# Unread identity transposes on TensorE at the head and before six waits, and one group's statistics moved behind its keys, in a two-phase graph-layer kernel

## The chip, the cores and the metric

One core of one Trainium2 chip runs the program. The metric is the time of one execution on the device in microseconds (us). The engines are named as the profile names them: PE (TensorE, matrix products and transposes into PSUM), DVE (VectorE), ACT (ScalarE), POOL (GpSimd) and SP (SyncE, which here only issues DMAs). PEld is the loading of the stationary operand on PE. The profile gives the clock that PE was granted as a share of full speed: 1.00 is 2.4 GHz, 0.50 is 1.2 GHz.

## The reference

The reference is one layer over 12500 nodes with 256 features. Cut to what matters:

```python
xn  = layernorm(x)
# graph part: 4 heads of 64 features, the neighbour of node n is col[n]
xt  = xn @ weight
al  = softmax(leaky_relu(sum(xt[row]*attn_l) + sum(xt[col]*attn_r)), over heads)
gnn = broadcast(sum over heads of al[n, h] * xt[col[n], h])
# linear attention, 8 heads of 32
Q, K = elu(xn @ Wq) + 1, elu(xn @ Wk) + 1
msg = (Q @ (K^T @ V)) / (Q . sum(K) + eps);  msg = layernorm(msg @ Wm)
h   = relu(concat(xn, msg) @ W1) @ W2;       x = x + gnn + xn + layernorm(h)
# mixture of experts on z = layernorm(x): a shared three-layer net, 4 experts, top 2
x   = x + shared(z) + sum over the 2 best experts of weight * expert(z)
```

The attention's sum over all nodes has to be complete before the first message can be formed. That splits the kernel in two phases.

## The kernel before

The nodes are cut into 25 groups (`NG`): 24 of 512 nodes (4 tiles of 128 rows) and a last one of 212 (2 tiles of 106). Every engine has its own instruction stream, written out by hand and ordered by semaphores; an engine executes its stream in that order, so a wait holds back all that is written behind it.

**The head** brings in group 0 and the first weights: DVE takes statistics of the rows (`stats`, `aggregate`), POOL turns them into scale and shift (`rstd`), ACT normalizes (`p1_norm`, result `xn1`), PE transposes (`p1_transpose`), ACT and DVE split the result in a high and a low part (`x1T_hi`, `x1T_lo`).

**Phase 1** then takes one group `v` a turn. PE's turn is: keys (`p1_k`, which needs `x1T_lo` of the group), transposes of group v+1 (which need `xn1` of v+1), and for each of two pairs of tiles the node tables (`p1_table`) and the sum of keys times rows of the group before (`p1_kx`, which needs POOL's `xr_lo` and `k_lo`). ACT's turn is: exponential of the keys (`kf`), copy of the transposed group v+1 (`x1T_hi`), two table copies (`xts`), normalization of group v+2. DVE's turn is: `xr_hi`, the statistics of group v+2 (`p1_stats`), the two operations on `kf`, `x1T_lo` of v+1, `k_hi`. POOL's turn is: `xr_lo`, `rstd` of group v+2, `k_lo`.

**The seam** between the phases (240 to 345 us) finishes the sum (`kx`), turns it (`kxT`), forms `kvT`, its product with `Wm` and a folded W1 weight, and runs turns 0 to 2 of phase 2 in an order of their own (`turn0`, `turn1`, and `phase2` with `second=True`).

**Phase 2** takes one group a turn: W1, W2, message, gating, shared net and experts. `w2_pair(i, 1)` waits for the four expert activations `e1` of ACT.

Each product of two fp32 operands is done as three products of parts in a faster type (`split_mm`, lines 282 to 284).

Of the kernel before, what the change touches and what calls it, by code (L numbers as in the profile page):

```python
# [20 lines left out]
P = 128  # L21
# [3 lines left out]
NG = -(-N_NODES // GR)  # L25
# [39 lines left out]
def gps_layer(nc, A):  # L65

    ctx = ExitStack()
    with ctx:
# [59 lines left out]
        ident = sb("ident", [P, P])  # L128
# [124 lines left out]
        psum = ctx.enter_context(nc.psum_tensor("psum", [P, 8, BANK], F32))  # L253
# [232 lines left out]
        def _(pe):  # L486
            def transposes(src, b, done, norm=None, before=0, t=T):
# [7 lines left out]
                                            ident[0:R, 0:R])  # L495
                last.then_inc(S[done], 1)

            def tile(t, c, j):
                return t[:, c, j * R:(j + 1) * R]

# [8 lines left out]
            def p1_transpose(v, par):  # L509
                if due(v):  # L510
                    pe.wait_ge(S["x1T"], v)
                transposes(xn1[par], 0, "x1t", "xn1", T * v, tiles(v))
# [36 lines left out]
            def phase1(v, par, kx=True, more=True):  # L549
                p1_k(v, par)  # L550
                if more:
                    p1_transpose(v + 1, 1 - par)
                for pair in range(2):
                    p1_table(v, par, pair)
                    if kx:
                        p1_kx(v - 1, 1 - par, pair, first=isinstance(v, int) and v == 1)

            def hidden(name, chunk, o, b, x, n=CK, t=T):

                for c in range(n):  # L560
                    last = split_mm(pe, colT(b, t=t), (wslice(w_hi, name, chunk + c, o * P, P),
                                                       wslice(w_lo, name, chunk + c, o * P, P)),
                                    (x[0][:, c, 0:t * R], x[1][:, c, 0:t * R]), c == 0, c == n - 1)
                return last
# [15 lines left out]
            def p2_expand(i, bank=6):  # L580
                pe.wait_ge(S["den_rows"], i + 1)
                for q in range(CK):
                    pe.matmul(colT(bank + q, t=tiles(i)), den_sel[:, q, :], rdenT[:, 0:tiles(i) * R], start=True,  # L583
                              stop=True).then_inc(S["dx"], 1)
# [11 lines left out]
            def w1_part(half, o, b, x, t=T):  # L596

                for c in range(CK):
                    k = 2 * half + c
                    last = split_mm(pe, colT(b, t=t),  # L600
                                    (wslice(w_hi, "W1", k, o * P, P), wslice(w_lo, "W1", k, o * P, P)),
                                    (x[0][:, c, 0:t * R], x[1][:, c, 0:t * R]), k == 0, k == 3)
                return last
# [6 lines left out]
                return last  # L610

            pe.wait_ge(S["ident"], 1)
            for half, done in enumerate(("x1t_first", "x1t")):
                for j in range(2):
                    pe.wait_ge(S["xn1"], 2 * half + j + 1)
                    for c in range(CK):
                        last = pe.transpose(psum[:, 4 * half + c, j * R:(j + 1) * R],
                                            xn1[0][:, 2 * half + j, c * P:(c + 1) * P], ident[0:R, 0:R])
                last.then_inc(S[done], 1)
            pe.wait_ge(S["wk_split"], 1)  # L620
            pe.wait_ge(S["x1T_first"], 1)
            first_k(0)
            pe.wait_ge(S["x1T"], 1)
            first_k(1).then_inc(S["k_mm"], 1)
            p1_transpose(1, 1)
            pe.wait_ge(S["w_split1"], 1)
            for pair in range(2):
                p1_table(0, 0, pair)
            phase1(1, 1)
            steps(pe, phase1, 2, NG - 2)  # L630
            phase1(NG - 2, (NG - 2) % 2)
            phase1(NG - 1, (NG - 1) % 2, more=False)
            pe.wait_ge(S["w_later"], 16 * LATER_LOADS)
            for o in range(4):
                for c in range(CK):
# [7 lines left out]
                p1_kx(NG - 1, (NG - 1) % 2, pair, last=True)  # L643


            pe.wait_ge(S["kxs"], 1)
            pe.wait_ge(S["xts"], 2 * NG)
            for c in range(CK):
                for q in range(CK):
                    last = pe.transpose(psum[:, 4 + c, q * P:(q + 1) * P], kx[:, q, c * P:(c + 1) * P], ident[:])  # L650
            last.then_inc(S["kxt_mm"], 1)
            pe.wait_ge(S["kden"], 1)
            p2_den(0)
            pe.wait_ge(S["kxT"], 1)
# [3 lines left out]
                                     kxT[:, c, q * P:(q + 1) * P], start=c == 0, stop=c == CK - 1)  # L658
            last.then_inc(S["kv_mm"], 1)
            w1_part(0, 0, 4, (xT_hi[0], xT_lo[0]))  # L660
            p2_expand(0)
            pe.wait_ge(S["kvT"], 1)
            for q in range(CK):
# [8 lines left out]
            def w2_pair(i, pair):  # L672

                if pair == 0:
                    pe.wait_ge(S["s1_relu"], 2 * (i - 1))
                else:
                    pe.wait_ge(S["e1_relu"], 4 * (i - 1))
                for j in (2 * pair, 2 * pair + 1):
                    for k in range(4):
                        last = split_mm(pe, rowt(0, j), (tile(h_hi, k, j), tile(h_lo, k, j)),  # L680
                                        (wslice(w_hi, "W2", k), wslice(w_lo, "W2", k)), k == 0, k == 3)
                last.then_inc(S["w2"], 1)
# [19 lines left out]
            def phase2(i, par, second=False):  # L702
# [29 lines left out]
                for e in range(EXPERTS):  # L732
                    if e == 1:
                        pe.wait_ge(S["s1_relu"], 2 * (i - 2) + 1)
                        pe.wait_ge(S["lg"], i - 1)
                        pe.transpose(psum[0:R, 5, 0:P], logitsT[:], ident[:]).then_inc(S["lt_mm"], 1)
                    hidden("eW1", 2 * e, 0, E1_BANKS[e], zT).then_inc(S["e1_mm"], 1)
                pe.wait_ge(S["h_lo"], 2 * i)
                for pair in range(2):
                    w2_pair(i, pair)  # L740
                pe.wait_ge(S["gate_rows"], i - 1)
                pe.transpose(psum[:, 5, 0:R], flat(scale_rows), ident[0:R, 0:R]).then_inc(S["scale_t"], 1)  # L742
# [514 lines left out]
        def _(dve):  # L1257
# [25 lines left out]
                now = slice(0, t * R)  # L1283
                tt(x1T_lo[par][:, :, now], colT(0, 2, t), x1T_hi[par][:, :, now], ALU.subtract).then_inc(S["x1T"], 1)

            def phase1(v, par, more=2):
                if due(v - 1):
                    dve.wait_ge(S["kx"], v - 1)
                t = tiles(v)
                dve.wait_ge(S["xn1"], xn_done(v + 1))  # L1290
                if isinstance(v, int) and v < 2:
                    dve.wait_ge(S["xr_ones"], 1)
                dve.tensor_copy(xr_hi[par][:, 0:t, 0:C], xn1[par][:, 0:t, :]).then_inc(S["xr_hi"], 1)
                if more >= 2:
                    p1_stats(v + 2, par)
                dve.wait_ge(S["k_exp"], v + 1)
                k = kf[par][:, 0:t, :]
                ts(k, k, 1.0, None, ALU.min)
                dve.drain()
                stt(k, rows4(2, t), 1.0, k, ALU.add, ALU.max).then_inc(S["kf"], 1)  # L1300
                if more >= 1:
                    p1_lowT(v + 1, 1 - par)
                dve.drain()
                dve.tensor_copy(k_hi[par][:, 0:t, :], k).then_inc(S["k_hi"], 1)

            dve.wait_ge(S["x_first"], 32)
            stats(LX[0], (0, 1), lambda j: xb[0][:, j, :])
# [21 lines left out]
            dve.tensor_copy(wx_hi[:, :, 0:XA_W], wx_raw[:])  # L1329
            dve.drain()  # L1330
            tt(wx_lo[:, :, 0:XA_W], wx_raw[:], wx_hi[:, :, 0:XA_W], ALU.subtract).then_inc(S["w_split1"], 1)
            phase1(0, 0)
            phase1(1, 1)
            steps(dve, phase1, 2, NG - 3)

# [76 lines left out]
            for q in range(CK):  # L1412
                at = kden[:, q, :].rearrange("p (d n) -> p d n", n=MIX_HEADS)[:, :, q * per:(q + 1) * per]
# [582 lines left out]
```

## Time and profile before

| | us |
|---|---|
| median of 3 runs | 1332.97 (1332.23 to 1333.31) |
| profiled execution, own time | 1329.47 |
| its span from first to last instruction | 1327.7 |
| PE busy | 1294.9 (98%) |
| DVE busy | 1045.5 (79%) |
| ACT busy | 751.7 (57%) |
| POOL busy | 646.3 (49%) |
| mean granted clock of PE | 0.993 |

Busy times are sums over the span of one profiled execution. Its own time is 1.8 us over its span and 3.5 us under the median of the runs without a profile.

### The profile page before, as it was taken

Reading aid. Unit: us, or ns where it says so; the run is one execution under the profiler, and the core shown is the slowest. Engines: PE = TensorE matmul, PEld = TensorE weight load, DVE = VectorE, ACT = ScalarE, POOL = GpSimd, SP = SyncE. Lnnn points to the kernel's source line nnn. Section 1 sums busy time; section 2 is a strip of 40 time slices with the busy share of each in tenths; the row PEclk is TensorE's granted clock in tenths of the full one; section 3 lists DMA queues with packets and bytes.
Section 4 is the critical chain, followed back from the end, with each engine's and each line's share of the span. In section 5 each row is a group of like instructions: output and inputs, shape, how many; then the busy total and the mean of one; then the engine's idle time right before and its main releaser. Section 6 shows DMA issues by size and latency. Waiting matters only on the chain.

```text
span 1327.7 us, 25928 instructions
## 1 busy us (share of the span) xinstructions
PE 1294.9 (98%) x8730; PEld 1122.8 (85%) x8730; DVE 1045.5 (79%) x2383; ACT 751.7 (57%) x1520; POOL 646.3 (49%) x721
## 2 busy tenths in 40 slices
PE   6999999898999999999999999999999999999998
PEld 6999999776888888888888888888888888888876
DVE  6887777878778787787878788787877878787765
ACT  4555555344557565565646565575645656565654
POOL 6777777636344443444343453444434453434421
PEclk9999999899999999999999999999999999999999
DMA  6787767522122312122021220222111220212000
GB/s 207 241 288 246 250 224 236 150 61 71 28 69 68 80 45 59 56 80 80 25 79 56 80 76 28 68 67 80 46 58 56 80 80 24 80 56 71 25 16 24
DMA packets 65459, 123.23 MB, mean 93 GB/s; under 512 B 31725, under 2 KB 36176, under 8 KB 65422
## 3 DMA queue, kind: packets, MB, share of 16 engines
q1 hardware_dynamic: 57422, 109.25, 25.5%
q0 software_dynamic: 8000, 13.53, 4.4%
q8 instruction: 19, 0.31, 0.1%
q14 instruction: 18, 0.15, 0.0%
HBM read 70.41 MB, written 52.32 MB: 92 GB/s over the span
## 4 chain that ended last, share of the span: by engine, by line
PE 89%; DVE 5%; ACT 2%; issue 1%; DVEq 1%; POOL 1%; DMA 0%; POOLq 0%; SPq 0%; ACTq 0%
PE psum L282 26%; PE psum L284 25%; PE psum L283 25%; PE psum L698 3%; PE psum L494 3%; PE psum L751 1%; PE psum L689 1%; PE psum L576 1%; PE psum L761 1%; PE psum L583 1%; PE psum L505 1%; DVE s_lo L1580 0%; DMA xb<-in_x 0%; DVE mT_lo L1553 0%; DVE qm L1547 0%
## 5 line engine op out<-in xcount | busy, mean ns | idle before, releaser
L1904 POOL TENSOR_TENSOR h_lo<-relu,h_hi 128x1024 fp32r<-128x1024 f32 (+1 forms) x50 | 124.0, 2481 | 170.6 <-ACT h_hi L1027 170.6
L282 PE MATMUL psum<-w_hi,h_hi 128*128 128x256 f32 x588 | 166.2, 283 | 3.6 <-ACT e L1038 3.1
L284 PE MATMUL psum<-w_hi,h_lo 128*128 128x256 f32 x588 | 165.8, 282 | 0.0
L283 PE MATMUL psum<-w_lo,h_hi 128*128 128x256 f32 x588 | 165.6, 282 | 0.0
L1904 POOL TENSOR_TENSOR s_lo<-relu,s_hi 128x512 fp32r<-128x512 f32 x23 | 29.7, 1293 | 206.7 <-ACT s_hi L1140 206.7
L282 PE MATMUL psum<-z_hi,w_hi 128*128 128x512 f32 (+1 forms) x300 | 121.7, 406 | 1.3 <-DVE z_lo L1673 1.0
L1060 ACT ACTIVATE mT_hi<-qm 128x1024 fp32r<-128x1024 f32 x23 | 24.4, 1062 | 170.5 <-DVE qm L1547 170.5
L282 PE MATMUL psum<-xT_hi,w_hi 128*128 128x512 f32 (+1 forms) x300 | 118.6, 395 | 0.2 <-DVE relu L1620 0.2
L1898 POOL DMA_INDIRECT xg<-table_xt,idx x100 | 100.0, 1000 | 35.6 <-issue 31.9
L284 PE MATMUL psum<-z_hi,w_lo 128*128 128x512 f32 (+1 forms) x300 | 116.2, 387 | 0.0
L284 PE MATMUL psum<-xT_hi,w_lo 128*128 128x512 f32 (+1 forms) x300 | 116.2, 387 | 0.0
L283 PE MATMUL psum<-xT_lo,w_hi 128*128 128x512 f32 (+1 forms) x300 | 116.1, 387 | 0.0
L283 PE MATMUL psum<-z_lo,w_hi 128*128 128x512 f32 (+1 forms) x300 | 116.0, 387 | 0.0
L282 PEld LDWEIGHTS psum<-w_hi,h_hi 128*128 128x128 f32 x588 | 111.3, 189 | 5.4 <-ACT e L1038 3.3
L283 PEld LDWEIGHTS psum<-w_lo,h_hi 128*128 128x128 f32 x588 | 112.6, 191 | 0.9
L1900 POOL DMA_INDIRECT ag<-table_al,idx x100 | 97.8, 978 | 30.5 <-issue 30.5
L284 PEld LDWEIGHTS psum<-w_hi,h_lo 128*128 128x128 f32 x588 | 111.2, 189 | 0.0
L1038 ACT ACTIVATE e<-psum,e_bias 128x512 f32<-128x512 f32 (+1 forms) x100 | 67.7, 680 | 49.8 <-PE psum L284 48.8
L1520 DVE SCALAR_TENSOR_TENSOR base<-xb,rn,b_bc 128x256 f32<-128x256 f32 x98 | 92.0, 981 | 0.2 <-issue 0.2
L1032 ACT ACTIVATE scaleT<-psum 32x128 fp32r<-32x128 f32 x98 | 26.4, 269 | 113.8 <-PE psum L742 112.9
L282 PE MATMUL psum<-mT_hi,w_hi 128*128 128x512 f32 (+1 forms) x200 | 80.0, 400 | 2.9 <-DVE mT_lo L1553 2.9
L284 PE MATMUL psum<-mT_hi,w_lo 128*128 128x512 f32 (+1 forms) x200 | 78.1, 390 | 0.0
(279 smaller groups left out, 4242.9 us busy)
## 6 DMA issues: line engine op xcount, KB each, us to landing
xb<-in_x SPq DMA_DIRECT2D x47, 448.0 KB, 4.0
xT_hi_table<-x1T_hi SPq DMA_DIRECT2D x25, 512.0 KB, 2.9
xT_lo_table<-x1T_lo SPq DMA_DIRECT2D x25, 512.0 KB, 3.6
xT_hi<-xT_hi_table SPq DMA_DIRECT2D x25, 512.0 KB
xT_lo<-xT_lo_table SPq DMA_DIRECT2D x25, 512.0 KB
table_xt<-xts SPq DMA_DIRECT2D x24, 455.0 KB, 3.0
out<-xmid SPq DMA_DIRECT2D x24, 448.0 KB
xb<-in_x SPq DMA_DIRECT2D x47, 64.0 KB, 4.1
```

What stands on the lines that cost most here:

```text
L282: pe.matmul(out, wh, xh, start=first, stop=False)
L283: pe.matmul(out, wh, xl, start=False, stop=False)
L284: return pe.matmul(out, wl, xh, start=False, stop=last)
L494: last = pe.transpose(psum[:, b + c, j * R:(j + 1) * R], src[:, j, c * P:(c + 1) * P], ident[0:R, 0:R])
L698: last = pe.matmul(psum[m * HEAD_CH:(m + 1) * HEAD_CH, 2 + q, 0:t * R], second_w[:, e, :], e1[:, e, 0:t * R], start=True, stop=True)
L1032: last = act.activation(scaleT[0:QUAD, j * R:(j + 1) * R], psum[j * QUAD:(j + 1) * QUAD, 5, 0:R], ACT.Copy)
L1038: act.activation(e1[:, e, 0:t * R], colT(bank, t=t), ACT.Relu, bias=e1_bias[:, e:e + 1]).then_inc(S["e1_relu"], 1)
L1060: act.activation(mT_hi[:], qm[:], ACT.Copy).then_inc(S["mT_hi"], 1)
L1520: last = stt(base[:, j, :], xb[par][:, j, :], rn2[par][:, 0, j:j + 1], b2_bc[:], ALU.mult, ALU.add)
L1898: pool.indirect_dma_start(xg[par][:, j, :], None, table_xt.ap(), bass.IndirectOffsetOnAxis(idx[par][:, 1, j:j + 1], 0)).then_inc(S[f"gath{ ...
L1900: pool.indirect_dma_start(ag[par][:, j, :], None, table_al.ap(), bass.IndirectOffsetOnAxis(idx[par][:, 0, j:j + 1], 0)).then_inc(S[f"gath{ ...
L1904: ptt(out, src, hi, ALU.subtract).then_inc(S[done], 1)
```

## The change

`keep_clock(n, bank)` issues n transposes of the identity matrix into a PSUM bank. Nothing reads their result, and they wait for nothing of their own. They are put at ten places of PE's stream: 38 as soon as the identity exists, 8 after each half of group 0's transposes, 8 ahead of the wait for the split of the table weights, and then 9, 14, 7, 6, 9 and 24 at the seam, ahead of the waits for POOL's `k_lo`, `kxs`, `kden`, `den_rows`, `h_lo` and `e1_relu`. On DVE, `p1_stats` of group 2 goes from behind `xr_hi` of group 0 to behind `k_hi` of group 0. All other turns are as before.

```diff
+            def keep_clock(n, bank, at=0):
+
+                for _ in range(n):
+                    pe.transpose(psum[:, bank, at:at + P], ident[:], ident[:])
+
...
             pe.wait_ge(S["ident"], 1)
+            keep_clock(38, 6)
             for half, done in enumerate(("x1t_first", "x1t")):
...
                 last.then_inc(S[done], 1)
+                if half == 0:
+                    keep_clock(8, 6)
+            keep_clock(8, 6)
             pe.wait_ge(S["wk_split"], 1)
...
             p1_transpose(1, 1)
+            keep_clock(8, 6)
             pe.wait_ge(S["w_split1"], 1)
...
-            phase1(NG - 1, (NG - 1) % 2, more=False)
+            p1_k(NG - 1, (NG - 1) % 2)
+            for pair in range(2):
+                p1_table(NG - 1, (NG - 1) % 2, pair)
+                if pair == 0:
+                    keep_clock(9, 1)
+                p1_kx(NG - 2, NG % 2, pair)
...
+            keep_clock(14, 1)
             pe.wait_ge(S["kxs"], 1)
...
             last.then_inc(S["kxt_mm"], 1)
+            keep_clock(7, 1)
             pe.wait_ge(S["kden"], 1)
...
             w1_part(0, 0, 4, (xT_hi[0], xT_lo[0]))
+            keep_clock(6, 5)
             p2_expand(0)
...
+                if second:
+                    keep_clock(9, 3)
                 pe.wait_ge(S["h_lo"], 2 * i)
                 for pair in range(2):
+                    if second and pair == 1:
+                        keep_clock(24, 3)
                     w2_pair(i, pair)
...
-            def phase1(v, par, more=2):
+            def phase1(v, par, more=2, stats_last=False):
...
-                if more >= 2:
+                if more >= 2 and not stats_last:
                     p1_stats(v + 2, par)
...
                 dve.tensor_copy(k_hi[par][:, 0:t, :], k).then_inc(S["k_hi"], 1)
+                if more >= 2 and stats_last:
+                    p1_stats(v + 2, par)
...
-            phase1(0, 0)
+            phase1(0, 0, stats_last=True)
             phase1(1, 1)
```

The stream of PE at the head, before the change, begins with the transposes of group 0 (`xn_0`):

```order
L617 MATMUL psum<-ident,xn_0 128x128 [waits s_xn1,s_ident]
L617 MATMUL psum<-ident,xn_0 128x128
L617 MATMUL psum<-ident,xn_0 128x128 [waits s_xn1]
L617 MATMUL psum<-ident,xn_0 128x128
L617 MATMUL psum<-ident,xn_0 128x128 [waits s_xn1]
```

With the change the same place reads:

```order
L501 MATMUL psum<-ident 128x128 [waits s_ident]
L501 MATMUL psum<-ident 128x128 x37
L623 MATMUL psum<-ident,xn_0 128x128 [waits s_xn1]
L623 MATMUL psum<-ident,xn_0 128x128
L623 MATMUL psum<-ident,xn_0 128x128 [waits s_xn1]
L623 MATMUL psum<-ident,xn_0 128x128
L501 MATMUL psum<-ident 128x128 x8
L623 MATMUL psum<-ident,xn_0 128x128 [waits s_xn1]
```

The 38 identity transposes wait for the identity alone, and group 0's transposes keep their waits for `xn1` behind them.

PE's stream at the end of phase 1, before, goes from the last key product (`k_hi`, `k_lo`) to the turning of the sum `kx` and on to the denominators (`kden`):

```order
L284 MATMUL psum<-xr_hi,k_lo 128x258
L650 MATMUL psum<-ident,kx 128x128 [waits s_xts,s_kxs]
L650 MATMUL psum<-ident,kx 128x128 x3
L576 MATMUL psum<-qf,kden 32x128 [waits s_q,s_kden]
L576 MATMUL psum<-qf,kden 32x128 x7
L657 MATMUL psum<-w_raw,wv 128x128 [waits s_kxT]
```

With the change:

```order
L284 MATMUL psum<-xr_hi,k_lo 128x258
L501 MATMUL psum<-ident 128x128 x14
L666 MATMUL psum<-ident,kx 128x128 [waits s_xts,s_kxs]
L666 MATMUL psum<-ident,kx 128x128 x3
L501 MATMUL psum<-ident 128x128 x7
L581 MATMUL psum<-qf,kden 32x128 [waits s_q,s_kden]
L581 MATMUL psum<-qf,kden 32x128 x7
L674 MATMUL psum<-w_raw,wv 128x128 [waits s_kxT]
```

Fourteen and seven identity transposes stand ahead of the two waits; nothing else moved.

DVE's stream in the turn of group 0, before, from the low part of the table weights (`wx_lo`) to the `xr_hi` of group 1 (`xn_1`):

```order
L1331 TENSOR_TENSOR wx_lo<-wx_raw,wx_hi 128x2x264
L1293 CAST xr_hi<-xn_0 128x4x256 [waits s_xr_ones,s_xn1]
L1262 BN_STATS bn_x<-xb 128x6 [waits s_rs_x1,s_x0]
L1262 BN_STATS bn_x<-xb 128x6 x3
L1267 BN_AGGR mv_x<-bn_x 128x2 x4
L1298 TENSOR_SCALAR kf<-kf 128x1024 [waits s_k_exp]
L1300 SCALAR_TENSOR_TENSOR kf<-psum,kf 128x1024
L1284 TENSOR_TENSOR x1T_lo<-psum,x1T_hi 128x1024 [waits s_x1T_hi]
L1304 CAST k_hi<-kf 128x1024
L1293 CAST xr_hi<-xn_1 128x4x256 [waits s_xr_ones,s_xn1]
```

With the change:

```order
L1355 TENSOR_TENSOR wx_lo<-wx_raw,wx_hi 128x2x264
L1315 CAST xr_hi<-xn_0 128x4x256 [waits s_xr_ones,s_xn1]
L1320 TENSOR_SCALAR kf<-kf 128x1024 [waits s_k_exp]
L1322 SCALAR_TENSOR_TENSOR kf<-psum,kf 128x1024
L1306 TENSOR_TENSOR x1T_lo<-psum,x1T_hi 128x1024 [waits s_x1T_hi]
L1326 CAST k_hi<-kf 128x1024
L1284 BN_STATS bn_x<-xb 128x6 [waits s_rs_x1,s_x0]
L1284 BN_STATS bn_x<-xb 128x6 x3
L1289 BN_AGGR mv_x<-bn_x 128x2 x4
L1315 CAST xr_hi<-xn_1 128x4x256 [waits s_xr_ones,s_xn1]
```

The statistics of group 2 (`mv_x`) have gone behind four operations, two of which wait for ACT. The streams of ACT, POOL and SP are the same as before.

## Rows read from the trace of the kernel before

**Rows 1.** Stretches: length, busy PE, PEld, DVE, ACT, POOL (instructions); clock; DMA share, GB/s.

```profile
40.00:240.00 200.00, 200.00 (x1693) 199.82 (x1693) 154.94 (x290) 113.50 (x214) 146.19 (x144) 1.00 0.76 247
345.00:1278.00 933.00, 932.65 (x6011) 786.72 (x6010) 747.47 (x1767) 546.95 (x1122) 408.50 (x462) 1.00 0.20 60
```

**Rows 2.** PE's longest waits, 240 to 345 us: total, times, longest.

```profile
PE psum L282 <- ACT e L1038: 3.1, 1, 3.1
...
PE psum L282 <- POOL k_lo L1874: 2.4, 1, 2.4
PE psum L576 <- DVE kden L1414: 1.2, 1, 1.2
PE psum L650 <- DVE kx L1409: 0.8, 1, 0.8
```

**Rows 3.** Three of the seam's four stretches at the lower clock, as rows 1.

```profile
245.10:248.50 3.40, 3.40 (x18) 3.40 (x18) 3.31 (x3) 0.28 (x2) 3.04 (x2) 0.51 0.21 66
258.80:262.30 3.50, 3.50 (x27) 2.92 (x18) 2.96 (x8) 0.00 (x0) 2.72 (x3) 0.51 0.36 68
...
333.90:337.30 3.40, 3.40 (x17) 3.40 (x17) 1.75 (x10) 0.09 (x1) 0.00 (x0) 0.50 0.02 5
```

**Rows 4.** First key products and a later stretch of them, as rows 1.

```profile
12.30:16.30 4.00, 4.00 (x19) 4.00 (x20) 3.78 (x7) 2.08 (x4) 0.79 (x3) 1.00 0.91 345
22.70:25.30 2.60, 2.60 (x23) 2.60 (x24) 2.44 (x6) 1.98 (x5) 1.93 (x1) 1.00 0.75 296
```

**Rows 5.** DVE in order of time, from 16.3 us on: start, length, instruction.

```profile
16.36 0.69 DVE L1293 CAST xr_hi<-xn 128x1024 fp32r<-128x1024 f32 x1
17.20 1.41 DVE L1262 BATCH_NORM_STATS2 bn_x<-xb 128x6 f32<-128x256 f32 x4 [0.16 <-issue]
18.68 0.38 DVE L1267 BATCH_NORM_AGGREGATE mv_x<-bn_x 128x2 f32<-128x6 f32 x4
18.98 1.09 DVE L1298 TENSOR_SCALAR kf<-kf 128x1024 f32<-128x1024 f32 x1
...
21.29 1.21 DVE L1284 TENSOR_TENSOR x1T_lo<-psum,x1T_hi 128x1024 fp32r<-128x1024 f32 x1
22.59 0.69 DVE L1304 CAST k_hi<-kf 128x1024 fp32r<-128x1024 f32 x1
...
26.76 0.75 DVE L1298 TENSOR_SCALAR kf<-kf 128x1024 f32<-128x1024 f32 x1 [0.43 <-ACT kf L969]
```

**Rows 6.** POOL: xr_lo of group 0, then group 2's scale chain, first and last.

```profile
17.12 2.40 POOL L1870 TENSOR_TENSOR xr_lo<-xn,xr_hi 128x1024 fp32r<-128x1024 f32 x1 [3.87 <-DVE xr_hi L1293]
19.48 0.65 POOL L1825 TENSOR_TENSOR veps_x<-mv_x,eps 128x4 f32<-128x4 f32 x1
...
21.86 0.20 POOL L1832 TENSOR_TENSOR rn<-nmean_x,rs_x 128x4 f32<-128x4 f32 x1
```

**Rows 7.** ACT: normalization of group 2 and exponential of group 1's keys.

```profile
22.60 2.07 ACT L944 ACTIVATE xn<-xb,rn,rs_x 128x256 f32<-128x256 f32 x4
25.70 1.03 ACT L969 ACTIVATE kf<-psum 128x1024 f32<-128x1024 f32 x1 [1.02 <-PE psum L284]
```

**Rows 8.** PE: transposes of group 2 and the table behind them.

```profile
25.50 1.03 PE L494 MATMUL psum<-ident,xn 128*128 128x128 f32 x8
26.29 0.37 PE L282 MATMUL psum<-wx_hi,x1T_hi 128*128 128x264 f32 x1
```

**Rows 9.** The seam's denominators on PE, and what stands around them on DVE.

```profile
254.45 1.23 DVE L1389 TENSOR_SCALAR qf<-psum 128x1024 f32<-128x1024 f32 x1 [1.81 <-PE psum L284]
...
258.55 0.90 PE L576 MATMUL psum<-qf,kden 128*32 128x128 f32 x16 [1.23 <-DVE kden L1414]
...
263.08 0.62 PE L583 MATMUL psum<-rdenT,den_sel 128*128 128x512 f32 x2
```

**Rows 10.** DVE's gate rows in turn 2, and PE's transpose that needs them.

```profile
335.18 0.17 DVE L1487 TENSOR_TENSOR scale_rows<-top_e,top_hi 128x16 f32<-128x16 f32 x1
...
336.75 0.41 PE L742 MATMUL psum<-ident,scale_rows 128*128 128x128 f32 x1
```

## The prediction

> **What bounds the kernel now.** I read the busy times by stretch first. In both long loops PE is busy all the time: 200.00 of 200 us in phase 1 and 932.65 of 933 us in phase 2, at the full clock [rows 1]. The reader is to see two things there: nothing in the loops can be gained by this change, which touches none of them, and whatever the head or the seam gains or loses comes out at the end whole, since PE works its stream off without a gap behind them. What is left is the head (0 to 22.6 us) and the seam (240 to 345 us). There I read PE's waits [rows 2] and the clock [rows 3]. The seam has waits of 3.1, 2.4, 1.2 and 0.8 us that the change touches, and behind them three stretches of about 3.4 us at half clock, in which PE is busy throughout; a fourth such stretch lies behind the wait for row_z of turn 2, which gets no transposes. The first key products at the head also run at the lower rate: 19 in 4.00 us, 0.21 us each, where a later stretch has 23 in 2.60 us, 0.113 each [rows 4]. (The clock column says 1.00 there; the rate of the products is what I trust.)
>
> **The price of the identity transposes.** The eight transposes of group 2 start at 25.50 and the table behind them at 26.29 [rows 8]: 0.10 us each at the full clock, so about 0.20 at half. I take the added ones at the same price. They are free where the wait behind them is longer.
>
> **Seam, wait for k_lo (9).** PE waits 2.4 us there [rows 2]; nine take 0.9 us, hidden by POOL's k_lo. Should the clock hold, the stretch 245.1 to 248.5 goes at full rate: half of 3.4 us, 1.70 us gained. Does it go through? PE's next consumer is DVE's qf, which stood idle 1.81 us for PE [rows 9], so 1.70 fits in. Term: −1.7. If nine don't hold the clock it is 0.
>
> **Seam, kxs, kden, den_rows (14, 7, 6).** The fourteen cost 1.4 us against a wait of 0.8 [rows 2]: the turning of kx starts 0.6 late. That eats into the next wait, 1.2 us, leaving 0.6 for seven transposes of 0.7 us: denominators at most 0.1 late. What the clock gives: the denominators take 0.90 us at half clock ahead of DVE [rows 9]; I take a third of it, 0.3, as back, since DVE starts on the last result. From there DVE's chain to den_rows sets the time (an addition, a reciprocal, a cast and four products, some 3.2 us), not PE's products, so their faster clock is worth only what PE was late behind that chain: PE reaches the expansion at 263.08 [rows 9]; den_rows is there some 0.35 before it by the same sum (258.55 + 0.94 + 3.2 = 262.7). Six transposes fit in the freed time. Term: −0.3 −0.35 = −0.65, bounds 0 and −1.7 (half of the whole stretch).
>
> **Seam, turn 2 (9, 24).** PE waits 3.1 us for ACT's e [rows 2]; 24 take 2.4, and the nine ahead of them push pair 0 by some 0.4 us into the same wait. Both are hidden, with 0.3 us to spare. The stretch 333.9 to 337.3 [rows 3] then runs at full rate: 1.7 at most. DVE's gate rows, needed next, are done at 335.35 and PE got to them at 336.75 [rows 10], so at that step 1.35 of 1.4 can be taken, and the expansion behind it adds 0.2. Term: −1.6.
>
> The fourth stretch I leave as it is. Seam in sum: −1.7 −0.65 −1.6 = **−3.95**.
>
> **Head, the clock.** The identity is there at about 1.75 us, group 0's rows at 9.1. 38 transposes need 38 × 0.20 = 7.6 us if the clock never rises (until 9.4, 0.3 late) and less if it does. If it has risen by 12.1, the 24 key products of group 0 are done at about 15.0 instead of 17.0, and ACT's exponential of them (1.03 us as for group 1 [rows 7]) starts at 15.4 behind its own normalization of group 1 and is done at 16.4. DVE is free at 17.05, where its xr_hi ends [rows 5]. So with the clock alone DVE would have gone on to the statistics as before and nothing would be gained: kf's first operation stood at 18.98 behind the statistics, not behind ACT. That is what the move of the statistics releases.
>
> **Head, the move.** I follow DVE's chain with the distances of rows 5. kf starts as xr_hi ends, at 17.0. It takes 0.75 as at 26.76, if it starts ahead of POOL's xr_lo (17.12), and 1.09 or more if behind. From kf to x1T_lo it was 2.31 us with the 1.09, so 1.97 with 0.75; from there to k_hi 1.30; from k_hi to the statistics 0.84, as between xr_hi and them; and 1.86 until mv_x is ready. So x1T_lo starts at 18.95 and ends at 20.15, k_hi starts at 20.25, the statistics at 21.1, and mv_x is ready at 22.95. Before, x1T_lo ended at 22.50 and mv_x was ready at 19.06 [rows 5]. So the keys of group 1 can start on PE at 20.4 (behind its second table) instead of 22.5, a gain of 2.1; and the statistics of group 2 come 3.9 us later. Who waits for them: POOL's scale chain (19.48 to 22.06 before, 2.6 us, and 2.15 if its first small operation takes 0.20 like its last and not 0.65 [rows 6]), then ACT's normalization of group 2 (2.07 [rows 7]), then PE's transposes of group 2, which had 0.8 us of slack (xn1 ready at 24.67 [rows 7], PE there at 25.50 [rows 8]). Now: 22.95 + 0.1 + 2.6 + 2.07 = 27.7 and two transposes: the table behind them at 27.95 against 26.29 [rows 8]. The gain of 2.1 at the keys is lost in a wait of about 2.3 us in front of these transposes, and **the head ends 1.65 us later**; with 2.15 for POOL's chain, 1.2 later. Queued behind ACT's late normalization is also its exponential for group 1, at 25.70 before [rows 7], now at 27.7; DVE's x1T_lo for group 2, five operations on, is there at 32, and PE needs it at 33.9, so that costs nothing more. POOL's k_lo of group 0 is behind the scale chain too, done at 28.1, needed at 29.4.
>
> And the clock: that wait has no identity transposes. PE stands from 23.4 to 25.7 and then does two transposes each half microsecond until 27.8. The wait of 2.4 us for k_lo was followed by 3.4 us at half clock [rows 2, 3]. The same here costs between 0.6 us (if most of the low stretch falls on the idle time) and 1.7. I take 1.3. Head in sum: 1.65 + 1.3 = **+2.95**, bounds +1.2 and +3.8.
>
> **Sum.** −3.95 + 2.95 = −1.0 us. On the profiled execution's 1329.5 that is 1328.5; on the median of the runs, 3.5 us higher, **1332.0**. About 0.2% (2.7 us) is what a measurement of this kernel can tell from no change, so this forecast is "the same". Its own range is −2.7 to +1.7, 1330.3 to 1334.7.
>
> **The rivals.**
>
> *The head costs little or gains; faster.* If POOL's chain takes the shorter 2.15 and the clock is not lowered in the new wait, the head is +1.2 and the sum −2.75 (1330.2). If xn1 of group 2 came in time for some reason that I don't see, the head would even be −2.1 and the sum −6 (1327). For it: the seam's gains rest on rows that are plain, and a shorter fourth stretch, by chance of its place, would add to them (up to 1.7). Against it: POOL's order puts the scale chain ahead of k_lo and ACT's puts the normalization ahead of kf, so nothing can overtake. It decides from a head below +1.3. Chance 0.28.
>
> *Nine are too few at the k_lo wait.* 0.9 us of work in 2.4 leaves 1.5 idle; the wait for kden (1.2, with 0.8 shortly ahead) was also followed by half clock. Then −1.7 is missing: +0.7, 1333.7. Also "the same". Chance 0.10.
>
> *The identity transposes don't keep the clock; slower.* The trace has no stretch with transposes alone from which this could be read: the eight of row_z in turn 2, spread out by ACT's pace, came just ahead of the fourth half-clock stretch. If they don't count, the 54 at the head run at 0.20: the 38 end at 9.4, and the 16 behind group 0's two halves add 3.2 us ahead of the first keys, so these start at about 15.0 instead of 12.1 and are at half rate. The keys end near 20, kf on DVE starts at 21.1 instead of 17.0, and all of the head comes 4.1 later than forecast: +2.95 + 4.1 = +7. The seam gains nothing. Sum +7: 1340. It decides if the first key products are at 0.21 us each. Chance 0.12. The Trainium skill, page "TensorE: Matmul & The Clock Gate", Part 4 on the PE-mode transpose, says that full clock doesn't engage for transposes because they don't count as busy in the same way; by that rule the outcome is this rival's.
>
> *The forecast.* Chance 0.50. Within it and the second rival some 0.04 lies above +2.7, for DVE's kf losing to POOL's xr_lo (2.4 us more at that step) together with the dear end of the clock.
>
> **Chances and range.** Faster 0.29 (first rival and a little of the forecast's edge), same 0.55, slower 0.16. The range takes in the first rival down to −4.6 and reaches towards the slower one, leaving out most of it: 1328.4 to 1336.5.
>
> **What would show it.** In the changed profile: a rate of 0.113 us a product in group 0's keys from 12.1 on (right for the clock at the head); the table of group 1 at 27.9, behind a wait of PE for ACT's xn of 2 us or more and then some 3 us at half clock (right for the head); no half clock at 245, 259 and 334, shifted by the head's delay (right for the seam). I am wrong if the transposes of group 2 wait for nothing, if a half-clock stretch stays behind one of the six waits, or if the first keys are still slow.

## The result and the profile after

The change made the kernel slower, by more than the prediction's range allows.

| | before | after |
|---|---|---|
| median of the runs (us) | 1332.88 (6 runs, 1331.71 to 1333.31) | 1339.93 (6 runs, 1338.09 to 1340.99) |
| ratio after / before, 95% interval | | 1.0053 (1.0040 to 1.0066) |
| profiled execution | 1329.47, span 1327.7 | 1340.16, span 1338.4 |
| mean granted clock of PE | 0.993 | 0.994 |

That is +7.05 us where −1.0 was forecast. One thing in this table matters for all that follows: the profiled execution of before is 2.2 us faster than the fastest of its runs, that of after lies in the middle of its own. In five of six sets of runs before took 1332.1 to 1332.9 us, in one (the four kernels h1 to h4) 1326.5, so each kernel is compared only with the runs of before in its own set.

The head first, PE of after in order of time (start, length, instruction; in brackets the idle time before it and what ended it):

```profile
1.73 7.07 PE L501 MATMUL psum<-ident 128*128 128x128 f32 x38 [1.73 <-POOL ident L1871]
...
9.94 1.04 PE L501 MATMUL psum<-ident 128*128 128x128 f32 x8
10.81 0.60 PE L623 MATMUL psum<-ident,xn 128*128 128x128 f32 x4
...
12.04 0.36 PE L282 MATMUL psum<-wk_hi,x1T_hi 128*128 128x256 f32 x1
...
26.39 2.07 PE L494 MATMUL psum<-ident,xn 128*128 128x128 f32 x8 [2.74 <-ACT xn L966]
28.12 0.57 PE L282 MATMUL psum<-wx_hi,x1T_hi 128*128 128x264 f32 x1
```

The eight between the halves go by in 0.87 us, 0.109 each. The first keys start at 12.04; 38 products in 4.00 us stand where [rows 4] had 19 in the same time (next fence, first row). Group 2's transposes wait 2.74 us for ACT's xn, and the table behind them starts at 28.12, for which 27.95 was forecast and [rows 8] has 26.29. Then comes the half clock, second row: PE at 0.54 for 3.7 us. Stretches of after, columns as in rows 1:

```profile
12.00:16.00 4.00, 4.00 (x38) 4.00 (x37) 3.71 (x7) 3.05 (x7) 0.14 (x1) 1.00 0.91 335
27.50:31.20 3.70, 3.65 (x18) 3.42 (x17) 2.45 (x3) 2.10 (x4) 3.58 (x8) 0.54 0.47 142
248.40:251.80 3.40, 3.40 (x31) 3.40 (x30) 3.31 (x3) 1.60 (x3) 3.04 (x2) 1.00 0.16 42
266.50:276.50 10.00, 5.33 (x16) 4.16 (x17) 4.50 (x11) 0.89 (x2) 3.01 (x4) 0.51 0.16 27
334.90:338.30 3.40, 3.40 (x10) 2.61 (x9) 3.23 (x2) 1.40 (x3) 3.24 (x3) 0.51 0.81 289
```

The third row is the stretch behind the wait for k_lo, 3.3 us later than in [rows 3]: full clock and 31 products, where half clock and 18 were. The last row is the fourth half-clock stretch of before, which the change leaves alone; it now stands behind a wait for logitsT and no longer behind the one for row_z. But 266.5 to 276.5 is new: ten microseconds at half clock with PE busy 5.33 of them. PE's waits in the seam of after, as rows 2:

```profile
PE psum L588 <- issue: 4.5, 1, 4.5
PE psum L494 <- ACT row_z L966: 2.4, 1, 2.4
PE psum L754 <- ACT logitsT L1125: 2.4, 1, 2.4
PE psum L682 <- issue: 2.4, 1, 2.4
PE psum L282 <- POOL k_lo L1898: 1.4, 1, 1.4
```

Against [rows 2]: the wait for e is gone and k_lo's is down from 2.4 to 1.4, and in front of the expansion (L588) and of the message's matrix (L682) stand 4.5 and 2.4 us that no row of before has. What they hang on is DVE, which itself gets PE's results late:

```profile
255.49 1.21 POOL L1922 DMA_INDIRECT xg<-table_xt,idx  x1 [1.02 <-issue]
260.50 0.64 PE L581 MATMUL psum<-qf,kden 128*32 128x128 f32 x16 [0.15 <-DVE kden L1438]
261.08 1.16 PE L674 MATMUL psum<-w_raw,wv 128*128 128x128 f32 x8
...
265.52 0.30 DVE L1520 TENSOR_SCALAR psum<-psum 128x128 f32<-128x128 f32 x1 [4.56 <-remote]
...
271.84 0.49 DVE L1780 TENSOR_TENSOR kvT<-psum,head_mask 128x128 f32<-128x128 f32 x2 [3.12 <-issue]
```

PE's sixteen denominator products start at 260.50 and take 0.64, and DVE, which waits for nothing else, starts on them at 265.52. "Remote" says that the profile has no event that released it. The eight products behind them, of which DVE makes kvT, were issued from 261.08 to 262.24, and DVE has them at 271.84, 9.6 us behind their end and after 3.12 us of standing idle. In the first profile of before DVE began 0.94 behind PE's start ([rows 9] for PE, and 259.49 for DVE). The first row is POOL's first gather of the seam. Its distance to DVE's start on the denominators, 10.03 us, comes back below.

### The profile page after: what moved, and what is told of

It reads as the page before. It is cut to its first block, busy times and chain, and to the rows that moved or that the text cites. A ratio compares the mean times of both kernels' runs of the same rounds, so it can differ in the third digit from the quotient of the medians.

```text
span 1338.4 us, 26189 instructions
## 1 busy us (share of the span) xinstructions
PE 1308.1 (98%) x8861; PEld 1135.1 (85%) x8861; DVE 1033.5 (77%) x2383; ACT 751.5 (56%) x1520; POOL 645.8 (48%) x721
## 4 chain that ended last, share of the span: by engine, by line
PE 90%; DVE 4%; issue 2%; ACT 2%; DVEq 1%; POOL 1%; POOLq 1%; another core or an unknown queue 0%; ACTq 0%
PE psum L282 26%; PE psum L284 25%; PE psum L283 25%; PE psum L716 3%; PE psum L494 3%; PE psum L773 1%; PE psum L707 1%; PE psum L588 1%; PE psum L783 1%; PE psum L581 1%; PE psum L510 1%; PE psum L501 0%; POOLq L1853 0%; ACT xn L966 0%; POOL k_lo L1898 0%
## 5 line engine op out<-in xcount | busy, mean ns | idle before, releaser
L1898 POOL TENSOR_TENSOR k_lo<-kf,k_hi 128x1024 fp32r<-128x1024 f32 x25 | 62.4, 2495 | 30.9 <-DVE k_hi L1326 30.9
```

Source lines behind the costliest of these rows:

```text
L1898: ptt(k_lo[par][:], kf[par][:], k_hi[par][:], ALU.subtract).then_inc(S["k_split"], 1)
```

## The experiments

Eighteen runs followed; f0 is before itself and i1 after itself. In the table, distances are (ratio − 1) × 1332 us with their 95% interval, against before of the same set. The distance between two medians, which the text gives in places, can differ from it by up to 1.1 us.

| kernel | what it is | us |
|---|---|---|
| e1 | change without the moved statistics | +5.7 (3.9 to 7.5) |
| e2 | moved statistics alone | +5.3 (3.6 to 7.2) |
| e3 | all of the seam's transposes alone | +3.1 (1.7 to 4.5) |
| e4 | all of the head's edits alone | +2.9 (1.7 to 4.1) |
| f1 / f2 | before / after without the seam's gathers | −6.0 / −2.3 |
| f3 | nine at k_lo alone | −0.9 (−2.1 to +0.3) |
| g1 | change without turn 2's transposes | +3.3 (1.9 to 4.9) |
| g2 | turn 2's transposes alone | +1.7 (0.5 to 2.9) |
| g3 | f3, half of group 1's gathers later | −3.5 (−4.8 to −2.1) |
| g4 | before, gathers behind den_rows | −0.5 (−1.7 to +0.7) |
| h1 | seam's first half (9, 14, 7, 6) alone | −2.3 (−4.4 to −0.3) |
| h2 / h3 | before / after with g3's gathers | −0.1 / +3.0 |
| h4 | head's transposes and 14 more | +0.7 (−1.5 to +2.8) |
| i1 | after once more | +7.7 (6.0 to 9.6) |
| i2 | h1 and g3's gathers | +0.7 (−0.5 to +1.9) |

**The change taken apart.** e1 puts the statistics back, e2 keeps only them, e3 keeps the seam, e4 the head:

```diff
-            phase1(0, 0, stats_last=True)
+            phase1(0, 0)
```

> All identity transposes stay, the statistics of group 2 go back to their old place. Both theories: the head's +3.3 us goes, since the normalization of group 2 is again in time; the keys gain nothing, because DVE's kf stands behind the statistics. Theory A (the stall between 260 and 277 us comes with the identity transposes of the seam, or with the length that they give PE's stream): the stall stays, about 1332.9 - 1.8 + 5.5 = 1336.6 us. Theory B (the stall comes because the seam is reached 3.3 us later and meets POOL's gathers and transfers otherwise): it goes, 1329.5 to 1331 us.

> Only the statistics of group 2 moved behind the keys of group 0, no identity transposes at all. The first keys stay slow (0.21 us each), kf starts at about 18.1, mv_x of group 2 is ready at about 24.1, its normalization at 28.9, so the table of group 1 starts at about 29.2 instead of 26.3: +2.9, and +1.3 for half clock behind the wait. Theory A: no stall at the seam, 1332.9 + 4.2 = 1337.1 us. Theory B: a stall of some 5 us at the seam as well, 1341 us or more.

> Only the seam's identity transposes (9, 14, 7, 6, 9, 24), head as before. By the sum of the prediction the seam gains 3.95: 1329 us. Theory A: the gain of 1.8 at the wait for k_lo stays and the stall of 5.5 comes, 1336.6 us, with half clock at the expansion. Theory B: no stall, 1329 to 1331 us.

> Only the head's identity transposes (38, 8, 8, 8) and the moved statistics, none at the seam. The head costs 3.3. Theory A with the seam's transposes as cause: no stall, 1332.9 + 3.3 = 1336.2 us. Theory B, or the length of PE's stream as cause: a stall at the seam, 1340 us or more.

Measured 1338.72, 1338.02, 1335.66 and 1335.48 us, before 1332.52. Theory A came within 1.0 us for e2, e3 and e4, B for none, and e1 missed both. The traces show why e1 was no better than after: with the fast first keys PE is done early and waits 1.80 us for x1T_lo, which hangs on DVE, and then runs group 1's keys at half clock:

```profile
22.94 0.39 PE L282 MATMUL psum<-wk_hi,x1T_hi 128*128 128x256 f32 x1 [1.80 <-DVE x1T_lo L1306]
```

```profile
22.90:26.50 3.60, 3.56 (x17) 3.56 (x18) 2.87 (x9) 1.65 (x4) 2.75 (x3) 0.54 0.76 292
```

Seventeen products in 3.6 us: e1's head ends 1.9 us late (PE is through its wait for k_lo at 246.32, before at 244.44). So the head's transposes alone buy nothing and lengthen a wait. For e2 the same point is 250.18, 5.7 late (4.2 expected), for e4 245.92, for e3 244.64. And e3 and e4 both had a late DVE at the denominators (4.55 and 2.92 us): the seam's transposes are not needed for it, so A's cause falls although its times were near.

**Is it in before too, and are the gathers part of it?** f0 is before, unchanged. f1 and f2 take POOL's gathers of groups 0 and 1 out of the seam:

```diff
-                gathers(0, range(T))
-                pool.wait_ge(S["idx1"], 2 * dma16(1, 1))
-                gathers(1, (0, 1))
...
+                    sp.dma_start(xg[n][:, j, :], table_xt.ap()[j * R:(j + 1) * R, :]).then_inc(S[f"ga{n}"], 16)
+                    sp.dma_start(ag[n][:, j, :], table_al.ap()[j * R:(j + 1) * R, :]).then_inc(S[f"ga{n}"], 16)
```

> The kernel before, unchanged, for a second profiled execution. All 18 runs of it lay at 1331.6 to 1334.6 us, the profiled one behind the prediction at 1329.5. Theory P (the late arrival of PE's results at the seam is there in most executions of every version, and the profile of before missed it): a wait of DVE of some 3 us for the denominators or the message, or of ACT in turn 2, span about 1331. Theory Q (it comes with the change only): the seam as in the first profile, the 3 us elsewhere.

> The kernel before, with POOL's 16 gathers of groups 0 and 1 at the seam replaced by 16 plain reads of the same size that SP issues (the rows read are the first of the table, so the neighbours' part of these two groups is another). If the gathers delay PE's results at the seam: 1332.5 - 3 = 1329.5 us, with no wait of DVE for the denominators. If they have no part: 1332 to 1333 us.

> The changed kernel with the same replacement. If the gathers are what turns the seam's gain into a loss: no wait of 4.5 us, the head's +3.3 and the seam's -2.5 to -4 stay, 1329 to 1330.5 us, 0 to +1 against the kernel before with the same replacement. If the stall has nothing to do with the gathers: 7 us above that kernel, about 1336.5 to 1339.5 us.

> The kernel before with the nine identity transposes ahead of k_lo alone. By the traces 1.8 us at the seam's entry are gained. If the late arrival of PE's results is there in any case: 1332.5 - 1.8 = 1330.7 us. If it comes with any transposes put into the seam: 1335.5 us as with all of them. If it takes the transposes next to the denominators (14, 7, 6): 1330.7 us too, and the trace shows whether DVE waits for the denominators.

Measured 1333.22, 1325.58, 1330.00 and 1331.18 us, before 1332.12. The second profile of before (f0), first gather, PE's products, DVE's start:

```profile
252.25 1.21 POOL L1898 DMA_INDIRECT xg<-table_xt,idx  x1 [1.02 <-SPq L441]
258.60 1.04 PE L576 MATMUL psum<-qf,kden 128*32 128x128 f32 x16 [1.23 <-DVE qf L1395]
262.25 0.30 DVE L1496 TENSOR_SCALAR psum<-psum 128x128 f32<-128x128 f32 x1 [2.99 <-remote]
```

So before has it, and the profile behind the prediction was an execution without it. f1 and f2 leave out the neighbours' rows of these two groups, as the expectation says. In f1, without the gathers, DVE starts 0.71 us behind PE, with no idle time that a row names:

```profile
256.75 0.64 PE L580 MATMUL psum<-qf,kden 128*32 128x128 f32 x16 [1.23 <-DVE kden L1418]
257.46 0.30 DVE L1503 TENSOR_SCALAR psum<-psum 128x128 f32<-128x128 f32 x1
```

f2 has the same 0.71. The DMA engines were no less busy in f1 than in f0 (a share of 0.41 against 0.35 from 256 to 262 us), so the bytes moved as such don't explain the delay.

Without these gathers before takes 6.0 us less and the changed kernel 9.4 (7.05 + 2.3), but not all of the 6.0 is theirs. In f1's trace the clock stayed full behind the wait for k_lo (2.4 us, as in f0), and DVE began qf at 252.65 instead of 254.50: those 1.85 us were won ahead of the place where the gathers take effect. And in turn 2, where f1 and f2 keep their gathers, ACT waits 3.57 and 3.78 us for a result of PE ("remote"). f2's time was as expected and its distance to f1 was not: the change still loses 4.4 us between the medians (3.7 by the table) without the seam's gathers, so they are not the only reason.

**Turn 2 and the gathers' place.** g1 and g2 take out or keep alone turn 2's transposes; g3 and g4 move gathers on POOL:

```diff
-                gathers(1, (0, 1))
                 pool.drain()
                 message_rstd(1)
-                gathers(1, (2, 3))
+                pool.wait_ge(S["idx1"], 2 * dma16(1, 1))
+                gathers(1, range(T))
```

> The changed kernel without the 9 and 24 identity transposes of turn 2. Theory S (in the usual execution PE comes so late to the wait for ACT's e that it is only 1.3 us long, and the 33 cost 3.7 us there): 1339.9 - 3.7 = 1336.2 us. The prediction's own term (they gain 1.6): 1341.5 us.

> The kernel before with the 9 and 24 identity transposes of turn 2 alone. Theory S: 1332.4 + 3.7 = 1336.1 us, with 24 transposes of some 2.8 us where ACT's e stood ready after 1.3 us. The prediction's term: 1330.8 us.

> The kernel before with the nine transposes ahead of k_lo, and POOL's four gathers of tiles 0 and 1 of group 1 moved behind its scale of the message of turn 0, to those of tiles 2 and 3. Theory P (PE's results reach DVE and ACT late only while POOL gathers): the first row of gathers ends at 262 instead of 267, kvT and the message come up to 3 us earlier, 1331.2 - 3 = 1328.5 us. If the gathers' number doesn't matter, or the later ones delay as much: 1331 to 1333 us.

> The kernel before with POOL's gathers of turn 0 held back until DVE has finished den_rows. Theory P: DVE no longer waits 3 us for the denominators (0.3 instead), and the delay moves to results of PE behind 263 us (kvT, g_hi, the first message); the time lies within 2 us of before either way, since DVE's group 0 features come later. If the late denominators have another cause than the gathers (PE's own stream or the clock): DVE waits for them as before, about 3 us.

Measured 1335.71, 1334.04, 1328.93 and 1332.71 us, before 1332.88. Turn 2's 33 transposes cost 3.7 us inside the change (7.05 − 3.3), 1.7 alone, where 3.7 was expected too. ACT's last e and PE around it, in after:

```profile
342.70 0.67 ACT L1060 ACTIVATE e<-psum,e_bias 128x512 f32<-128x512 f32 x1
```

```profile
343.70 2.78 PE L501 MATMUL psum<-ident 128*128 128x128 f32 x24
346.23 0.36 PE L282 MATMUL psum<-w_hi,h_hi 128*128 128x256 f32 x1
```

e is done at 343.37, before the first of the 24 starts. They hide nothing: they take 2.53 us and the nine ahead of them 0.91 (339.88 to 340.79), 3.4 together. In f0 the wait is 1.26 us, and no half clock follows it, so there is neither a cover for 24 nor a clock to keep:

```profile
339.64 0.38 PE L282 MATMUL psum<-w_hi,h_hi 128*128 128x256 f32 x1 [1.26 <-issue]
340.10 0.28 PE L282 MATMUL psum<-w_hi,h_hi 128*128 128x256 f32 x1
```

Behind the 3.1 us of [rows 2] stands one long operation of DVE, s_lo, ahead of the softmax on which ACT's e is queued. The same operation in the first profile of before, in h4 and h1 (both below) and in f0:

```profile
321.65 5.86 DVE L1580 TENSOR_TENSOR s_lo<-relu,s_hi 128x1024 fp32r<-128x1024 f32 x1 [0.82 <-ACT s_hi L1027]
```

```profile
321.37 5.83 DVE L1596 TENSOR_TENSOR s_lo<-relu,s_hi 128x1024 fp32r<-128x1024 f32 x1 [0.84 <-ACT s_hi L1041]
```

```profile
319.94 3.01 DVE L1595 TENSOR_TENSOR s_lo<-relu,s_hi 128x1024 fp32r<-128x1024 f32 x1 [0.34 <-ACT s_hi L1040]
```

```profile
332.19 2.40 DVE L1580 TENSOR_TENSOR s_lo<-relu,s_hi 128x1024 fp32r<-128x1024 f32 x1 [4.29 <-ACT s_hi L1027]
```

In the first two it started together with POOL's h_lo (321.67 and 321.36), and PE waited 3.10 us for e in both. In h1 it started 0.8 us behind h_lo (319.15), and e was ready when PE came. In f0 it started 3.4 us behind h_lo (328.74) and ended as long behind that start as in the first profile, 5.85 us. There the wait is shorter because PE is later: it began these products 6.65 us behind h_lo's start instead of 4.80, after ACT had waited 3.62 us for a result ("remote"). So the wait of 3.1 us needs two things at once, results in time and DVE and POOL starting together.

g4 holds the gathers back until den_rows. DVE then starts on the denominators after an idle time of 0.48 us. A wait of 4.03 us "remote" stands at the denominators of turn 1, where the gathers now are: PE issued them at 272.67, DVE is free for them at 276.62 and has them at 280.65, and ACT has one of 3.84 us next to it:

```profile
263.53 1.21 POOL L1898 DMA_INDIRECT xg<-table_xt,idx  x1 [12.65 <-DVE rdenT L1504]
```

```profile
259.39 0.30 DVE L1496 TENSOR_SCALAR psum<-psum 128x128 f32<-128x128 f32 x1 [0.48 <-PE psum L576]
...
280.65 0.30 DVE L1496 TENSOR_SCALAR psum<-psum 128x128 f32<-128x128 f32 x1 [4.03 <-remote]
280.71 1.08 ACT L1234 ACTIVATE w_hi<-psum 128x512 fp32r<-128x512 f32 x2 [3.84 <-remote]
```

The late results go where the gathers go. Whether it is the gathers' issue on POOL or their reads that matters, no run separates. g3, with fewer gathers in that stretch, is the fastest of the versions that leave nothing out, in the sets in which before took 1332 us.

**What remains, and the parts against each other.**

```diff
             for pair in range(2):
                 p1_table(0, 0, pair)
+            keep_clock(14, 6)
             phase1(1, 1)
```

is h4's addition to the head's transposes (with the statistics in their old place).

> The kernel before with the identity transposes of the seam's first half (9, 14, 7, 6) alone. Theory S (what they gain ahead of the denominators is swallowed, since the denominators reach DVE some 10 us behind POOL's first gather whatever PE does): within 1 us of before, about 1332.5 us. The prediction's terms (-1.7 - 0.65): 1330.2 us. If the 14, 7 and 6 cost something of their own: above f3's 1331.2 by what they cost, up to 1334.

> The kernel before with only POOL's four gathers of group 1 moved behind its message scale, no identity transposes. Theory P: most of the 4 us that g3 gained come from here, 1329 to 1330.5 us, and the nine transposes ahead of k_lo are worth 0 to 1.7. If the gain of g3 was the nine transposes': 1332.5 us.

> The changed kernel with the same move of the gathers. Theory P and S: the head's +3.2 and turn 2's +2 to +4 stay, the gathers' move gives 3 to 4: 1336 to 1337 us, 6 to 7 us above h2. If the late results were the only reason for the loss: 1331 us.

> The kernel before with the head's identity transposes (38, 8, 8, 8), the statistics in their old place, and 14 more ahead of the wait of 1.8 us for group 1's x1T_lo. In e1 that wait was followed by half clock over the keys of group 1, and the head ended 1.9 us late. If that is the cause: full clock there, the head ends where it did before, 1332 to 1333 us. If something else of the head's transposes costs: 1334.5 us.

Measured 1323.18, 1325.58, 1329.95 and 1327.90 us, before 1326.54. In this set before itself spread from 1323.15 to 1329.89, with 15 of 35 times up to 1325.2 and 17 from 1327.8 on. No trace of the set had late denominators, although h1 and h4 leave the gathers where they always are: h1's DVE starts 0.71 us behind PE. It isn't the chip either, since e1 to e4 ran on the same one, with before at 1332.52.

```profile
257.24 0.64 PE L581 MATMUL psum<-qf,kden 128*32 128x128 f32 x16
257.95 0.30 DVE L1511 TENSOR_SCALAR psum<-psum 128x128 f32<-128x128 f32 x1 [0.21 <-PE psum L581]
```

So the gathers don't suffice for the lateness; that they are needed rests on f1, f2 and g4. The two heaps of before look like turn 2's s_lo: from row_z's transposes to the gate rows' PE takes 25.6 and 25.9 us in the first profile and in h4 (1329.47 and 1329.13 us), 21.3 in h1 and h2 (1321.85 and 1324.72). For the runs without a profile this is not shown.

h1 gained 2.3 us (−4.4 to −0.3; 3.4 between the medians), for which the prediction had 2.35. With such heaps that agreement is loose, and the traces are the surer witness: PE is at the message's matrix at 261.79 in h1 and at 263.55 in the first profile of before, 1.8 us earlier. The change with moved gathers lost 4.4 us between the medians against before with the same move (h3 − h2; 3.2 by the table), less than the 6 to 7 expected. Against h2, PE is 3.7 us behind at k_lo in h3, 1.9 at the message's matrix and 4.6 at turn 2's gate rows: head +3.7, first half −1.8, turn 2 +2.7. h4's fourteen transposes fill e1's wait and the clock stays full over group 1's keys: 29 products in 3.6 us, k_lo at 244.54.

```profile
22.40:26.00 3.60, 3.34 (x29) 3.32 (x29) 2.92 (x7) 2.08 (x5) 2.51 (x1) 1.00 0.71 281
```

That accounts for e1's late head, and gains nothing: PE still waits 0.26 us for DVE there. The time of h4 can't be told from before.

> The changed kernel itself once more, since the last set of runs had before at 1326.5 us and PE's results in time at the seam. Theory P and S: if before is at 1326 to 1328 again, the changed kernel is at the head's +3.2, the first half's -2 to -3.4 (now not swallowed) and turn 2's +3.7 above it, so +3.5 to +5: 1330 to 1331 us; if before is at 1332 to 1333, it is 7 us above. If late results had no part in the 7 us, the distance is 7 us in either case.

> The version that the runs point to: the kernel before with the identity transposes of the seam's first half (9, 14, 7, 6) alone, and POOL's four gathers of group 1 moved behind its message scale. 3 to 4 us below before in either condition: about 1323 us where before is at 1326.5, about 1328.5 us where it is at 1332.5.

Measured 1339.16 and 1332.75 us, before 1332.29. The set was again one of late results, and i1's distance, 6.9 us between the medians, was that of the first measurement, as expected for such a set; whether it is smaller when PE's results come in time was not measured for the changed kernel itself, only for h3. i2 missed its expectation by 4 us. It is g3 with 14, 7 and 6 transposes more, and lies 4.2 us above it (+0.7 against −3.5):

```profile
252.22 1.21 POOL L1913 DMA_INDIRECT xg<-table_xt,idx  x1 [1.02 <-issue]
257.24 0.65 PE L581 MATMUL psum<-qf,kden 128*32 128x128 f32 x16
262.25 0.30 DVE L1511 TENSOR_SCALAR psum<-psum 128x128 f32<-128x128 f32 x1 [4.51 <-remote]
```

In g3 the first gather, PE's products and DVE's start are at 252.09, 257.11 and 259.15. PE is equally early, and DVE 3.1 us later. The two are from different sets, with before at 1332.9 and 1332.3 us.

## Why the prediction was wrong

**The price of the identity transposes** was right: 0.109 us each against 0.10.

**Head, the clock and the move: right.** The first keys run at 0.11 us from 12.04 on. The table of group 1 came at 28.12 (27.95 forecast), behind a wait of 2.74 us and with 3.7 us of half clock. PE passes the wait for k_lo 3.3 us later than before (247.73 against 244.44), where +2.95 was forecast. It isn't the same in every execution. The same head ended 2.4 us late in i1 and 2.6 in g1, and 1.5 in e4, where no half clock followed the wait of 2.75 us; the bounds +1.2 to +3.8 held all of them. The rival in which identity transposes don't keep the clock named 1340, which is the time measured, and was still wrong; the number is luck: its mark, first keys at 0.21 us, did not come. By that rule of the Trainium skill, page "TensorE: Matmul & The Clock Gate", Part 4, full clock doesn't engage for transposes; the trace disagrees for these fp32 transposes, with 54 identity and 8 data transposes ahead of keys at the full rate (38 products in 4.00 us).

**Turn 2, −1.6: wrong step.** "PE waits 3.1 us for ACT's e" was true of one execution in which PE's results were in time and s_lo met POOL's h_lo. In f0 the wait is 1.26 us with full clock behind it, and in after, h1 and h3 e was ready before PE came to it. The cover that made the transposes free wasn't there, and the half clock that they were to lift wasn't either. Measured: +3.7 within the change, +1.7 alone, and +2.7 by the traces of h3 and h2.

**Seam, k_lo, −1.7, and kxs, kden, den_rows, −0.65: right mechanism, gain not kept.** In after no half clock follows k_lo, and PE reaches the denominators only 1.9 us later than f0 while the head is 3.2 late: 1.3 us are won there. Where PE's results come in time, 1.8 us of the 2.35 are there at the message's matrix (h1 against before, h3 against h2). Where they come late, DVE gets the denominators 10.0 us behind POOL's first gather in after, e1, e3, g1, i1 and i2 alike, though PE issued them 5.0 us behind it each time. With the nine alone (f3, g3) and with none of the first half (g2, e2) PE issued them at 5.0 as well, and DVE got them at 7.1 to 7.2. So the 14, 7 and 6 put 2.9 us onto the denominators. Which of the three does it was not tried apart; the six stand behind the denominators in PE's stream. This is no term of the sum at all: the prediction asked what they cost PE, and not what they do to PE's results behind them.

**The sum.** Between f0 and after, both with late results, PE is 3.2 us behind at k_lo, 3.9 at the message's matrix, 2.9 at turn 2's logits and 6.6 behind the 24, and the spans differ by 6.9. Head +3.2, first half −0.3 instead of −2.35, turn 2 +3.7 instead of −1.6, and +0.3 behind it: together +6.9 instead of −1.0.

**The root** is the sentence that set the profiled execution 3.5 us under the median of the runs and went on with its waits. 2.8 us under the fastest of three runs was a sign that this execution was not of the kind that is timed. In f0 the waits for k_lo, kx and kden are the same 2.4, 0.8 and 1.2 us, but that for e is 1.26 instead of 3.1, and waits of 2.2 and 1.8 us for late results stand at the expansion and the message's matrix. The term for turn 2 rested on the first, and the 2.35 us of the first half were lost in the second.

What stays open: why PE's results reach DVE and ACT late during gathers, in some executions and not in others, and why transposes ahead of the denominators add to it. The traces show issue times and arrivals; a stall inside PE and a late signal look alike in them.

## What to carry to other kernels

Before filling a wait with unread work, take its length from several profiled executions: filler beyond the shortest of them is paid for, and a profile that is faster than every timed run describes another execution. Filler keeps the clock, but it pays only where PE's end is not set by another engine; a faster stretch ahead of such an engine lengthens the next wait and can lose the clock there (e1). Of this change at most the nine transposes at k_lo are worth keeping: alone they gave −0.9 us (−2.1 to +0.3), not clear of nothing, and in f1, g2 and e2 the clock stayed full there without them. With half of group 1's gathers moved behind the message scale they gave −3.5 us (g3). That move alone was measured only in the set without late results (h2, −0.1), so g3's gain is not divided between the two.

## What the hardware showed

While POOL's indirect gathers run, results of PE can reach DVE and ACT late. At the seam's denominators DVE stood idle for 1.5 to 4.6 us, with the arrival at 7.1 or 10.0 us behind the first gather; the products behind them reached DVE 9.6 us late in after. In f0 and e4 PE issued at 6.3 us behind it and the arrival was at 9.9 to 10.0. Without the gathers in that place (f1, f2, g4), and in the set h1 to h4 with them, DVE started 0.7 to 1.2 us behind PE's start. The half clock appeared behind waits of 1.8 us (e1) and 2.7 us (after) and stayed away behind 2.75 us (e4). Behind the same wait of 2.4 us at k_lo it appeared in the first profile of before, f0, e4, g4, h2 and h4 and stayed away in f1, g2 and e2: the length of the wait alone did not decide it. A DVE operation on 128x1024 elements took 5.86 us when it started together with one of POOL, and 3.01 us when it started 0.8 us behind it (h1).
